# Expert weights' rests on VectorE among the gates, marks in the rounded type, and second weights at the top of SBUF

## The reference

```
x = x + L0_attn(norm(x))            # 16 heads of 64, causal
x = x + L0_xattn(norm(x), ctx, ctx, mask)   # 16 heads of 64, cross attention
x = x + L0_ffn(norm(x), ...)        # routed experts, below
x = x + L1_attn(norm(x))            # linear attention
x = x + L1_xattn(norm(x), ctx, ctx)
x = x + L1_ffn(norm(x), ...)        # gated value and output experts
```

## Time and profile before

| | us |
|---|---|
| median of three runs | 3734.63 (3733.24 to 3734.75) |
| the profiled execution's own time | 3770.42 |
| its span | 3768.7 |
| TensorE busy (matmuls) | 3535.4 |
| VectorE busy | 2815.1 |
| ACT busy | 2067.1 |
| GpSimd busy | 460.0 |

### The profile page before, as it was taken

How to read it: one execution, slowest core, us unless ns; L and a number is a source line. 1 busy time by engine, 2 the same in 40 slices (tenths; PEclk the granted TensorE clock), 3 DMA queues, 4 the chain that set the end, 5 groups by cost and what they waited for, 6 DMA issues and landing times. The chain is left out here.

```text
span 3768.7 us, 92062 instructions
## 1 busy us (share of the span) xinstructions
PE 3535.4 (94%) x28674; PEld 2949.1 (78%) x28674; DVE 2815.1 (75%) x8955; ACT 2067.1 (55%) x6494; POOL 460.0 (12%) x599
## 2 busy tenths in 40 slices
PE   8999999899999999489967989999799999999999
PEld 6888888788888887389945666666688888888887
DVE  7666666677777776766657977888788888888886
ACT  6777777677777776335534648888433223232232
POOL 0000000000000000435578002222000000000000
PEclk9999999999999999689989999999899999999999
DMA  2000000110000000312211000000300000000000
GB/s 103 0 0 0 0 0 0 40 35 11 11 11 11 11 11 12 129 50 77 73 59 45 0 17 20 22 22 17 105 9 14 11 8 17 8 14 11 8 14 9
DMA packets 48158, 96.08 MB, mean 25 GB/s; under 512 B 7584, under 2 KB 21280, under 8 KB 47776
## 3 DMA queue, kind: packets, MB, share of 16 engines
q1 hardware_dynamic: 40640, 75.48, 6.0%
q0 software_dynamic: 6528, 17.83, 1.6%
q10 hardware_dynamic: 864, 1.19, 0.1%
HBM read 72.46 MB, written 22.02 MB: 25 GB/s over the span
## 5 line engine op out<-in xcount | busy, mean ns | idle before, releaser
L2416 DVE TENSOR_TENSOR f_zgT<-f_zT,f_ps_g 128x512 fp32r<-128x512 f32 x512 | 327.4, 681 | 15.4 <-PE f_ps_g L2248 11.4
L718 ACT ACTIVATE c_pr<-c_sm,c_nmx 128x256 f32<-128x256 f32 x512 | 254.5, 499 | 148.7 <-DVE c_nmx L550 148.7
L148 PE MATMUL f_ps_out<-f_out_rounded,f_zgT 128*128 128x256 f32 x1024 | 295.4, 288 | 1.3 <-DVE f_zgT L2416 1.3
L149 PE MATMUL f_ps_out<-f_out_rest,f_zgT 128*128 128x256 f32 x1024 | 289.4, 283 | 0.0
L150 PE MATMUL f_ps_out<-f_out_rounded,f_zgT 128*128 128x256 f32 x1024 | 288.0, 281 | 0.0
L2369 DVE TENSOR_TENSOR f_gv<-f_ps_v,f_gm 128x512 f32<-128x512 f32 x256 | 175.6, 686 | 143.1 <-PE f_ps_v L150 142.9
L718 ACT ACTIVATE a_pr<-a_sm,a_nmx 128x128 f32<-128x128 f32 (+1 forms) x512 | 227.1, 444 | 99.6 <-DVE a_nmx L550 99.6
L550 DVE CUSTOM_DVE_ANT_0 a_sm<-a_ps_s,causal 128x128 f32<-128x128 f32 (+1 forms) x512 | 152.3, 354 | 152.8 <-PE a_ps_s L416 152.8
L550 DVE CUSTOM_DVE_ANT_0 c_sm<-c_ps_s,c_mask 128x256 f32<-128x256 f32 x512 | 186.5, 420 | 87.9 <-PE c_ps_s L416 87.7
L2505 ACT ACTIVATE f_pr<-f_sm,f_nmx 128x128 f32<-128x128 f32 (+1 forms) x256 | 114.9, 449 | 193.2 <-DVE f_nmx L2389 193.2
L2514 ACT COPY f_prT<-f_ps_t 128x256 f32<-128x256 f32 x128 | 47.8, 373 | 287.3 <-PE f_ps_t L2217 287.3
(11 more groups left out here) (422 smaller groups left out, 11523.5 us busy)
## 6 DMA issues: line engine op xcount, KB each, us to landing
f_slot_out<-f_y SPq DMA_DIRECT2D x72, 128.0 KB, 1.7
c_ctx_stage<-in_ctxT SPq DMA_DIRECT2D x32, 256.0 KB, 2.8
f_w_whole<-in_f_w SPq DMA_DIRECT2D x15, 512.0 KB, 5.1
x_sb<-in_x SPq DMA_DIRECT2D x8, 512.0 KB, 7.3
c_mask_stage<-in_mask SPq DMA_DIRECT2D x16, 256.0 KB, 3.0
f_token_rows<-f_t SPq DMA_DIRECT2D x16, 256.0 KB, 3.3
x_mid<-x_sb SPq DMA_DIRECT2D x16, 256.0 KB, 2.0
f_xn<-x_mid SPq DMA_DIRECT2D x16, 256.0 KB, 2.6
```

The lines of the kernel that those rows point to most:

```text
L148: nc.tensor.matmul(out, sh, mh, start=start, stop=False, **kw)
L149: nc.tensor.matmul(out, sh, ml, start=False, stop=False, **kw)
L718: last = nc.scalar.activation(pr[:, r, i, 0:n], sm[:, j, i, 0:n], ACT.Exp, bias=nmx[:, j, i:i + 1], scale=-1.0, accum_out=sums[:, r, i:i + 1])
L2416: last = nc.vector.tensor_tensor(zgT[:, k % 2, r], zT[:, s % 2, r, :].bitcast(F32).unsqueeze(1).broadcast_to([P, 2, S]), ps_g[:].rearrange ...
```

## The change

1. GpSimd no longer subtracts the rests of the experts' weights. VectorE does: one piece in each turn of the gates from the third on, the last two behind the gates. ACT rounds in the same turns.
2. The order of the pieces becomes: gate, second weights of experts 1 to 7, first and second weights of expert 0, first weights of experts 1 to 7. Eight of them are loaded in the cross attention instead of two: the gate and w2 of expert 1 into the staging tensor, w2 of experts 2 to 7 (six pieces) into their places, which now lie at the top of SBUF, above what the cross attention uses. Nine pieces are left to be loaded in the experts' stage.
3. hot_row and hot_tile become fp32r. The first comparison goes to a new fp32 tile `marks`, which lies in the same place as hot_tile; the two tiles that borrowed room from the old ones borrow from it.
4. `owners` waits for count 43 (the cast of the owners' words) instead of 49, and stands behind `turn_rows(0)` on TensorE, behind `rest_x(0)` on VectorE and behind `round_x(0)` on ACT.

```diff
-        hot_row = sb("hot_row", [P, 2, GROUP, P], F32, choosing)
-        hot_tile = sb("hot_tile", [P, 2, GROUP, NT], F32, choosing)
+        hot_row = sb("hot_row", [P, 2, GROUP, P], F32R, choosing)
+        marking = ExitStack()
+        marks = sb("marks", [P, 2, GROUP, NT], F32, marking)
+        marking.close()
+        hot_tile = sb("hot_tile", [P, 2, GROUP, NT], F32R, choosing)
...
-            eng.wait_ge(made, CHOICES)
+            eng.wait_ge(made, OWNED)
...
-            pieces.load(sp, Pieces.STAGES, 4)
+            pieces.load(sp, early, early + 2)
             for b in range(B):
                 store_t(b)
-                pieces.load(sp, 4 + b, 5 + b)
+                pieces.load(sp, early + 2 + b, early + 3 + b)
...
-            pool.wait_ge(t_ready, B)
-            pool.wait_ge(pieces.split, 1)
-            pieces.rest_by_pool(nc, pool, 1, len(pieces.list))
...
-            regs, owner_of = owners(pe)
-            pe.wait_ge(pieces.split, len(pieces.list))
-
...
+            turn_rows(0)
+            regs, owner_of = owners(pe)
+            pe.wait_ge(pieces.split, len(pieces.list))
...
             for b in range(B):
                 rest_tT(b)
+                if b >= 2:
+                    pieces.rest(nc, dve, b - 1, b)
                 if b + 2 < B:
                     normalise(b + 2)
+            pieces.rest(nc, dve, B - 1, len(pieces.list))
...
-                nc.vector.tensor_tensor(hot_tile[:, g % 2], each(tile_of[:, at], NT), every(block_no[:], NT),
+                nc.vector.tensor_tensor(marks[:, g % 2], each(tile_of[:, at], NT), every(block_no[:], NT),
                                         ALU.is_equal).then_inc(tile_hot, 1)
...
-                nc.vector.tensor_tensor(hot_tile[:, g % 2], hot_tile[:, g % 2], each(token_no[:, token], NT),
+                nc.vector.tensor_tensor(hot_tile[:, g % 2], marks[:, g % 2], each(token_no[:, token], NT),
                                         ALU.mult).then_inc(hot_ready, 1)
...
-                if b % 2:
-                    pieces.round(nc, act, 1 + b // 2, 2 + b // 2)
+                if b >= 2:
+                    pieces.round(nc, act, b - 1, b)
             take_lT(B - 1)
+            pieces.round(nc, act, B - 1, len(pieces.list))
...
-            pieces.round(nc, act, 1 + B // 2, len(pieces.list))
...
+        EARLY = 8
+        order = [("w2", e) for e in range(1, 8)] + [("w1", 0), ("w2", 0)] + [("w1", e) for e in range(1, 8)]
...
+        above = ExitStack()
+        above.enter_context(nc.sbuf_tensor("f0_below_w2", [P, 23664], F32))
+        w2 = halves(above, "f0_w2", [8, 4, D])
+        above.close()
...
-            pieces["f0"].load(sp, 0, Pieces.STAGES)
+            pieces["f0"].load(sp, 0, EARLY)
```

More of the change, by code:

```diff
@@ L757, in _, with routed_experts @@
             steps(act, slot)
-def routed_experts(nc, c, tag, pieces, w1, w2, gate_w, b1, b2, norm_w, load_next):
+def routed_experts(nc, c, tag, pieces, early, w1, w2, gate_w, b1, b2, norm_w, load_next):
     E, HID, FC, TOPS = 8, 512, 4, 2
@@ L815, in routed_experts @@
         slot_f = sb("slot_f", [P, Q], F32, choosing)
-        tile_no = hot_row[:, 1].rearrange("p g m -> p (g m)")[:, 0:NT * (E - 1)].rearrange("p (n e) -> p n e", e=E - 1)
-        owner_f = hot_tile[:, 1, 0, :]
+        tile_no = marks[:].rearrange("p a g n -> p (a g n)")[:, 0:NT * (E - 1)].rearrange("p (n e) -> p n e", e=E - 1)
+        owner_f = marks[:, 1, 0, :]
         power = sb("power", [P, WORDS, PER], F32, choosing)
@@ L870, in routed_experts @@
         CHOICES = 49
-        SLOTS, PLACED = 37, 38
+        SLOTS, PLACED, OWNED = 37, 38, 43
         xt = lambda n: c.x[:, n:n + 1, :].rearrange("p a d -> p (a d)")
@@ L1063, in second @@
                 last.then_inc(y_ps, 1)
-            turn_rows(0)
             for n in range(NT + 2):
@@ L1208, in _ @@
             done(nc.vector.tensor_copy(owner[:], word_f[:]))
+            assert k == OWNED, k
             done(nc.vector.tensor_copy(slot_at[:].rearrange("p r n -> p (r n)"), slot_f[:]))
@@ L1217, in _ @@
             assert k == CHOICES, k
-            regs, owner_of = owners(dve)
             def rest_x(n):
@@ L1247, in _ @@
             rest_x(0)
+            regs, owner_of = owners(dve)
             for n in range(NT + 3):
@@ L1295, in _ @@
             nc.scalar.activation(ex[:], diff[:], ACT.Exp).then_inc(ex_ready, 1)
-            pieces.round(nc, act, 1 + B // 2, len(pieces.list))
-            regs, owner_of = owners(act)
             def round_x(n):
@@ L1320, in _ @@
             round_x(0)
+            regs, owner_of = owners(act)
             for n in range(NT + 1):
@@ L2711, in program @@
         flat = lambda ap: ap.rearrange("p a b m -> p (a b m)") if len(ap.shape) == 4 else ap.rearrange("p a m -> p (a m)")
[L2712 to L2715, removed]
+        EARLY = 8
+        order = [("w2", e) for e in range(1, 8)] + [("w1", 0), ("w2", 0)] + [("w1", e) for e in range(1, 8)]
+        f0_src = [flat(dram["f0_gate"])] + [flat(dram[f"f0_{name}"][:, e]) for name, e in order]
         room_f0 = ctx.enter_context(ExitStack())
         f0, load_f0_small = weights(room_f0, "f0", norm=[DC], b1=[32], b2=[8 * D])
+        above = ExitStack()
+        above.enter_context(nc.sbuf_tensor("f0_below_w2", [P, 23664], F32))
+        w2 = halves(above, "f0_w2", [8, 4, D])
+        above.close()
+        pieces["f0"].list += [(None, None, None, f0_src[0])]
+        pieces["f0"].list += [(None, None, flat(w2[2][:, e]), src) for (_, e), src in zip(order[:EARLY - 1], f0_src[1:])]
         def load_f0(sp):
             load_f0_small(sp)
-            pieces["f0"].load(sp, 0, Pieces.STAGES)
+            pieces["f0"].load(sp, 0, EARLY)
         with ExitStack() as room:
@@ L2739, in program @@
             w1 = halves(room, "f0_w1", [8, DC, 512])
[L2740 to L2743, removed]
+            expert = {"w1": w1, "w2": w2}
+            places = [tuple(flat(t[:]) for t in gate)] + [tuple(flat(t[:, e]) for t in expert[name]) for name, e in order]
             pieces["f0"].list[:] = [(*place, src) for place, src in zip(places, f0_src)]
-            routed_experts(nc, c, "f0", pieces["f0"], w1[:2], w2[:2], gate[:2], f0["b1"], f0["b2"], f0["norm"], load_l1)
+            routed_experts(nc, c, "f0", pieces["f0"], EARLY, w1[:2], w2[:2], gate[:2], f0["b1"], f0["b2"], f0["norm"], load_l1)
         room_f0.close()
```

## The result

The changed kernel takes 3712.45 us (median of four runs, 3710.68 to 3714.62) against 3734.46 before (3733.24 to 3734.75): a ratio of 0.994 with the 95% interval 0.9927 to 0.9953, 22.0 us less. The forecast was 3711.9 us, 22.7 less.

The account below looks back on a forecast made before the run. TensorE, busy 94% of the span, bounds the kernel, so gains come only where it idles. Terms -25.3, +6.9, -8.3, -0.8 and +4.8 sum to -22.7 us: 3734.6 becomes 3711.9 us, range 3703 to 3721.

Parts of the forecast that it names:

- cross attention: Cross attention: six early weight loads delay batch 1's context, ACT and then TensorE wait; 4.8 us lost, bounds 0 and 8.
- gates, to the logits: Experts' gates: with the rests VectorE sets 2.65 us a turn; logits 6.9 us later, bounds 0 and 19.5.
- choice: Experts' stage, choice of slots: without GpSimd's rests VectorE needs 18.9 us instead of 44.2, 25.3 less.
- marks: Experts' stage: rounded products take one instruction each, VectorE sets the pace; 21.9 us instead of 30.2, 8.3 less.
- ids to the first product: Start of the experts: first rows turned before owners(), register loads overlapped; first product 0.8 us earlier, bounds 0 and 4.
- Rival 4: Choice of slots: GpSimd is not the cause of the slowness, so it stays at 44.2 us; 3737.2 us, chance 0.03.
- The pair of L1142: Choice before the change: same instruction and shape takes 1.99 us, then 0.42 in GpSimd's pause; sign against GpSimd.
- the quarter price: Experts' marks: by the four-pass rule a rounded product costs 0.11 us, saving 9.1 instead of 8.3, 23.5 in all.
- Rival 2: Cross attention: TensorE's idleness also lowers its clock for 6 us, 3 us lost; 3714.9 us, chance 0.12.
- the likeliest case: Whole kernel: the forecast itself, all terms as priced, 22.7 us less, 3711.9 us; chance 0.45.
- Rival 5: Cross attention: slipped context makes TensorE wait in each of 120 following slots; 3748 us at 0.3 a slot, chance 0.03.
- The sum against the profiled execution: Whole kernel: terms built on the profiled 3770.4 us gave 3747.7; the median's 35.8 us lower level was taken as unaffected.

Follow-up runs that it names:

- two early: Changed kernel with only the gate and one second weight loaded in the cross attention, six others among the gates again: 3704.62 us, repeated 3707.88.
- rests in VectorE's waits: Changed kernel, batch 1's context issued before next-stage loads, last two rests moved into VectorE's idle waits: 3736.25 us, where before takes 3765.2.

## Why the prediction was right

By its terms, in microseconds, from the two traces; the stage starts with SP's first load, and the measured column is after less before:

| term | forecast | measured |
|---|---|---|
| cross attention | +4.8 | +6.4 |
| gates, to the logits | +6.9 | +6.7 |
| choice | -25.3 | -25.3 |
| marks | -8.3 | -8.3 |
| ids to the first product | -0.8 | -1.7 |
| sum | -22.7 | -22.2 |

(0.2 us of the stage's delay were there before the early loads, which gives the 22.0 of the traces.)

Two terms were off, by 1.6 and 0.9 us, and in opposite directions; that the sum comes within half a microsecond is partly luck. The three large terms were right by their mechanism.

**Choice.** Rival 4 is out. The pair of L1142 in the trace of before was enough to price it; the run with the rests back on GpSimd shows it. (Ahead of the hole GpSimd made eight rests, not seven; nothing hangs on it.)

**Gates.** 2.57 us a turn against my 2.65, with two waits for ACT's rounding of 0.5 us that I had not seen. VectorE is the pace, as said. That normalise no longer waits for the stores of t is true of this trace, but not for the reason that I gave: the run with the rests on GpSimd has six loads fewer and waits for stores seven times, and two early, with all loads back in the gates, has no such wait in its second profile. I read it as the slower pace that gives the stores their time. (By its own times the term is 6.8 and not 6.9.)

**Marks.** An instruction costs about 0.215 us from start to start, in either kernel: the same for either type at these 72 columns, and half as many. So the quarter price that I had worked out from the Trainium skill (FP8 and Floating Point Precision, TensorE Precision Notes) was wrong here, and my 0.21 right. It changes little, because VectorE sets the pace. At the same clock, behind the hole of the cross attention, rounded products of 256 columns also start 0.21 us apart (786.35 and 786.56), so 72 columns are not what costs it, and no run here shows the ratio of the types where columns do.

**Owners.** The term was mis-sized. The rows land 4.2 us after the cast of ids, as taken (4.35). From there to the first product I had 3.4 us, and it is 2.7 (1605.99 to 1608.71). The register loads take at most 2.1 us instead of 2.4, and they stand behind the turning of one tile only. Nearly all of them lie beside ACT's and VectorE's work, which ends at 1608.06.

**Cross attention.** The mechanism stands, by three runs: the context waits in the queue. The size was off. The context landed at 784.1, not at 782.5, because the stretch from 776 on moved 342 to 358 GB/s, not 397; so ACT's wait was 6.3 us instead of 5.1. When SP issued it hardly matters: in the run with the marks in fp32 the context left earlier, at 773.51, and ACT waited 6.4 us.

The hole in TensorE was 4.8 us, as forecast, but by luck. I had TensorE stop at the transposes of pr, with 0.2 us to spare. It stopped before them, at the first product of the context (785.54 above), which needs VectorE's subtraction. In the kernel before, VectorE and TensorE in order of time:

```profile
778.18 0.68 DVE L586 TENSOR_TENSOR c_ctxT<-c_ctx_stage,c_ctxT 128x512 fp32r<-128x512 f32 x1
...
780.30 0.28 PE L148 MATMUL c_ps_kv<-c_ctxT,c_w_rounded 128*128 128x256 f32 x1
```

The subtraction was done at 778.86, so 1.4 us of the slip cost nothing. A wait that was 1.2 us too short and a slack that was 1.2 us too small gave the right hole.

The rest of the 6.4 is the clock: the twelve products behind the hole take 2.7 us where they took 1.4, at 0.62 from 784 to 788. Rival 2, in half its size, came on top of the likeliest case. Rival 5 did not come: TensorE idles nowhere later in the cross attention.

**The sum against the profiled execution** was a weak step: I took the 35.8 us between 3770.4 and the median as the profiler's cost, but the changed kernel's profiled run, 3712.69 us, is no longer than its others, and some 30 us of the 35.8 are the idle times of the linear attention. It did no harm only because no term lay there.

## What to carry to other kernels

When the same VectorE instruction has two durations in one trace, look at what GpSimd does meanwhile before moving anything. A transfer issued early is paid for by the transfers behind it in its queue; issue first what a working engine will wait for next, and give the large loads what is left. Work moved to an engine that has idle time is cheap only up to the point where that engine sets the pace, and the last instalment, behind the loop, is paid in full.

## What was unexpected in the hardware

While GpSimd subtracts, even a VectorE subtraction of 32 columns takes 2.21 us instead of 0.19.

The same load at the same place in SP's queue (the first piece of weights, behind about 1 MB) took 0.43 us to issue in the kernel before, 1.66 in the changed one and 0.52 to 1.79 in other runs with the same loads; what decides it is open.

The clock can fall once more some 10 us after the experts' first product, and it does so when TensorE is already busy again behind 2.1 us of idleness. In three stretches of 2 us from 1611.12 on, the run with rests in VectorE's waits has 0.82, 0.50 and 0.83, with TensorE busy throughout. Nine of the fourteen profiles show such a fall, both of before among them, and five do not, the changed kernel among them; two early has it in one of its two profiles. In the five the clock had risen to 1.00 later after the first product (4.8 us and more, an estimate from the clock of stretches of 2 us, against at most 4.5 in the nine). The fall costs about 1 us: from the first product to the loads at the end of the stage it is 260.0 us in two early without it and 260.9 with it. Both profiles of before need 262.7, and what the other 1.8 us are is open.

And on one chip the linear attention of every version takes 30 us longer.
